# A graph convolution followed by a routed expert network: the first steps of the last stage in another order, with filler matmuls, and 16 instead of 20 edge rows within the pass over x

## What is computed

```python
# x: 12500 x 256, 200000 edges (src, dst, edge_weight), dst sorted
x = x + segment_sum(layernorm(x) @ W [src] * edge_weight, dst) + b      # graph convolution
h = layernorm(x)                                                        # 12500 tokens, D = 256
# routing: ONE vector of logits for all tokens, since B = 1
logits = mean(h, tokens) @ Wr + br            # 8 experts
w = softmax(softmax(logits) * scale)          # scale: capacity
top_w, top_i = top_k(w, 2); top_w = softmax(top_w)
y_e = gelu(h @ W1[e] + b1[e]) @ W2[e] + b2[e] # F = 512; only the two chosen e count
x = x + layernorm(top_w[0] * y_{i0} + top_w[1] * y_{i1} + h)
```

## Time and profile before

| what | value |
|---|---|
| median of 3 runs | 2423.52 us (2422.5 to 2423.78) |
| the profiled execution, its own time | 2425.1 us |
| span of the profile | 2423.2 us |
| PE busy | 2205.2 us (91%) |
| POOL busy | 1617.9 us (67%) |
| DVE, ACT busy | 1030.0 us (43%), 1168.0 us (48%) |
| instructions | 40839 |

### The profile page before, as it was taken

One profiled execution on the slowest core, in us unless ns is written; L12 is line 12 of the kernel. 1 busy time (PEld: TensorE's weight loads), 2 busy tenths in 40 slices (PEclk: granted clock), 3 DMA queues, 4 the chain that ended last, 5 costly groups with the idle time before them and its releaser, 6 DMA issues. The chain is left out here.

```text
span 2423.2 us, 40839 instructions
## 1 busy us (share of the span) xinstructions
PE 2205.2 (91%) x9799; PEld 1696.4 (70%) x9800; DVE 1030.0 (43%) x2967; ACT 1168.0 (48%) x3163; POOL 1617.9 (67%) x1627
## 2 busy tenths in 40 slices
PE   2488899999999999999899999899989979999998
PEld 1367667776667667666677676676766767998897
DVE  7984232322223222232323222322321255889896
ACT  3578667656555545444434343232242116565663
POOL 6777777777777777777777777777777751333432
PEclk9899999999999999999999999999999989999999
DMA  9855565658555655555556556555555542233321
GB/s 374 322 175 155 157 178 166 189 163 271 181 175 171 186 174 177 178 184 168 158 173 189 183 169 191 173 167 187 171 173 179 183 134 83 102 105 127 118 77 59
DMA packets 218864, 414.72 MB, mean 171 GB/s; under 512 B 36227, under 2 KB 130230, under 8 KB 218728
## 3 DMA queue, kind: packets, MB, share of 16 engines
q0 software_dynamic: 75008, 204.90, 28.3%
q1 hardware_dynamic: 143288, 206.10, 26.1%
q10 hardware_dynamic: 432, 2.40, 0.3%
HBM read 332.61 MB, written 80.65 MB: 171 GB/s over the span
## 5 line engine op out<-in xcount | busy, mean ns | idle before, releaser
L533 POOL DMA_INDIRECT G<-xr_d,SRC x1467 | 1395.4, 951 | 447.3 <-issue 296.9
L1024 DVE TENSOR_SCALAR OH<-CST,DL,WR 128x128 f32<-128x128 f32 x1564 | 565.9, 367 | 1279.1 <-PE ps L1337 970.3
L1337 PE MATMUL ps<-G,OH 128*128 x3128 | 743.4, 391 | 104.0 <-DVE OH L1024 75.6
L1337 PEld LDWEIGHTS ps<-G,OH 128*128 128x128 f32 x3128 | 594.2, 194 | 262.5 <-issue 184.4
L1327 PE MATMUL ps<-W2u,H 128*128 128x256 f32 x1792 | 412.3, 389 | 20.3 <-issue 19.3
L1327 PEld LDWEIGHTS ps<-W2u,H 128*128 128x128 f32 x1792 | 344.5, 195 | 88.2 <-issue 41.3
L1316 PE MATMUL ps<-YU,W1u 128*128 128x512 f32 x896 | 394.0, 592 | 1.5 <-issue 1.1
L1316 PEld LDWEIGHTS ps<-YU,W1u 128*128 128x128 f32 x896 | 170.1, 190 | 192.6 <-issue 183.7
L733 ACT ACTIVATE YE<-ps 128x512 f32<-128x512 f32 x112 | 66.8, 596 | 478.4 <-PE ps L1327 478.4
L726 ACT ACTIVATE H<-ps,b1a 128x512 f32<-128x512 f32 x224 | 153.9, 687 | 208.0 <-PE ps L1316 207.7
L612 ACT ACTIVATE OHX<-OHT,WR 128x128 f32<-128x128 f32 x194 | 67.5, 394 | 223.6 <-PE ps L1337 223.6
(11 more groups left out here) (204 smaller groups left out, 2338.5 us busy)
## 6 DMA issues: line engine op xcount, KB each, us to landing
W1u<-in_W SPq DMA_DIRECT2D x56, 512.0 KB
W2u<-in_W SPq DMA_DIRECT2D x56, 512.0 KB
y_d<-YE SPq DMA_DIRECT2D x56, 512.0 KB, 5.4
G<-xr_d,SRC POOLq DMA_INDIRECT x1467, 2.9
x_d<-X SPq DMA_DIRECT2D x98, 128.0 KB, 2.4
yt_d<-YT SPq DMA_DIRECT2D x98, 128.0 KB, 2.3
XR<-in_x SPq DMA_DIRECT2D x97, 128.0 KB, 3.0
XS<-in_x SPq DMA_DIRECT2D x24, 512.0 KB, 19.1
```

The lines of the kernel that those rows point to most:

```text
L533: e.indirect_dma_start(out=G[0:rows(s), s % RING, :], out_offset=None, in_=x if s < FRESH else xr_d, in_offset=bass.IndirectOffsetOnAxis(a ...
L1024: e.tensor_scalar(OH[:, s % OHR, :], iota, DL[:, s:s + 1], WR[:, s + 1:s + 2], ALU.is_equal, ALU.mult).then_inc(s_oh, 1)
L1337: e.matmul(ps[:, 0, 0:D], OH[:, r, :], Gf[:, bass.ds(g + r * D, D)], start=False, stop=True, skip_group_check=True).then_inc(s_main, 1)
```

## The change

Seven edits, in two places of the program.

In the pass over x, `between` puts 3 and 2 rows of edge statistics behind groups 18 and 22 instead of 5 and 4.

In the last stage: ACT's `high(1)` stands in the chain of the routing, behind `XH`; DVE's `low(1)` behind the low parts of W1; ACT's and DVE's steps for `W2h`, `W2l`, `bias_rows` and the first `normal2` come one to several hidden tiles later; PE's first four hidden tiles are done in pairs (high, high, low, low) and no longer all four high parts first; and 6 and 12 filler matmuls of 128x512 (`keep_warm`), whose result is never read, are put on PE before and behind the routing's small matmuls.

```diff
@@ the pass over x
-        between = [1 if 6 <= g < 12 else 5 if g == XBUF else 4 if g == XBUF + LOTS[0] else 1 if g > XBUF else 0 for g in range(NG)]
+        between = [1 if 6 <= g < 12 else 3 if g == XBUF else 2 if g == XBUF + LOTS[0] else 1 if g > XBUF else 0 for g in range(NG)]
@@ ACT
             e.activation(XH[:, :], X1[:, t % 4, :], ACT.Identity, bias=NR[:, t:t + 1], scale=R1[:, t:t + 1]).then_inc(s_xh, 1)
+            high(1)
             e.wait_ge(s_route, 9)
@@
-                    if k == 0 and i in (1, 3):
-                        high_w2(i // 2)
-                    if i == 3 and k + 1 < len(post):
+                    if k == 0 and i in (2, 3):
+                        high_w2(i - 2)
+                    if i == 3 and 1 <= k and k + 1 < len(post):
                         high(k + 1)
-                    if i == 4 and k - 1 in pre_of:
+                    if i == 1 and k == 1 or i == 4 and k - 1 in pre_of:
                         normal2(n)
                         n += 1
-                    if i == 6 and k < len(post):
+                    if i == 6 and 1 <= k < len(post):
@@ DVE
             for h in range(2):
                 low_w1(1, two, h)
+            low(1)
@@
-                    if k == 0 and i in (1, 3):
-                        low_w2(i // 2)
-                    if k == 0 and i == 4:
+                    if k == 0 and i in (2, 4):
+                        low_w2(i // 2 - 1)
+                    if k == 0 and i == 7:
                         bias_rows()
@@
-                    if i == 4 and k + 1 < len(post):
+                    if i == 4 and 1 <= k and k + 1 < len(post):
                         low(k + 1)
@@ PE
+            def keep_warm(n):
+                for _ in range(n):
+                    e.matmul(ps[:, 7, :], ones_r[:, :], YTh[:, 0, 0, :], start=True, stop=True, skip_group_check=True)
@@ behind the last multiplication by Wsb
+            e.wait_ge(s_ye, 2 * UNITS + 2)
+            e.wait_ge(s_yth, 1)
+            keep_warm(6)
@@ behind the transposes of XH
             ins.then_inc(s_tr, 1)
+            keep_warm(12)
@@
-            for i in range(HB):
-                up_high(0, i)
-            for i in range(HB):
-                up_low(0, i)
+            for i in range(0, HB, 2):
+                for j in range(i, i + 2):
+                    up_high(0, j)
+                for j in range(i, i + 2):
+                    up_low(0, j)
```

## The result

The changed kernel takes 2414.97 us (median of 7 runs, 2413.79 to 2418.25) beside 2423.78 (7 runs) for the one before on the same chip: a ratio of 0.9963 (0.9951 to 0.9974), 9.0 us less. On another chip five runs gave 2410.75 beside 2421.71, 0.9959 (0.9945 to 0.9972), 9.9 us less. Gains in us are worked out from the ratio throughout (its interval is some 3 us to either side); the medians alone can differ by 1 us from it. The forecast was 2410.8, 12.7 less: right in direction and within its range, 2.8 to 3.7 us too good.

The account below looks back on a forecast made before the run. POOL's gathers set the pace up to about 1983 us, PE's own work in the steady part from 2020. From the 2423.5 median, 1.8 (pass) and 10.9 (fill) come off: 2410.8 us, range 2408.5 to 2415.5.

Parts of the forecast that it names:

- The pass: Pass over x: fewer edge rows let POOL's stalled gather near 98 us restart 1.8 us earlier; bounds 0 and 3.2.
- both arms: Work needed before PE's `begin` (98.13): ACT's scaling and `AS`, ready at 95.2; PE's first edges and event, 96.3.
- The gather moves with it, 101.33 - 1.8 = 99.5: POOL's gather released by PE's seventh edge row starts 1.8 us earlier, as `begin` does; the floor is 98.15.
- The first rival: The pass gives its whole stall: ACT's arm decides and gives 2.9, at most 3.2 us; total 2409.5; 20%.
- The fill: Start of the last stage: `up(1, 1)` starts at 2008.7 instead of 2019.57, a gain of 10.9 us.
- `W2s` lands at 2001.1 and 2002.6 ..., the evictions ask for it at 2001.2 and 2003.5: In the fill, both `W2s` loads land 4.2 us after issue, before ACT's evictions need them.
- The wait for `YTl` goes: In the fill, PE's 4.06 us wait for `YTl` of group 1 disappears, with `high(1)` and `low(1)` moved earlier.
- I take it that the clock stays at 2.4 GHz: With the fillers, PE's clock does not halve from the routing through the fill; half clock had cost about 3 and 2.6.
- the third rival: The clock falls in the routing anyway; the twelve fillers take 5.1, ending 1.8 late; 2411.9 or 2413.8 us; 17%.
- Then the fill no longer runs its first 16 matmuls at 0.427 each: PE's first fill matmuls avoid half clock, at which one of 512 columns takes 0.427 us; at full clock 0.235.
- The steady loss of 1.5 us or so by late `YTl` stays: Behind the fill, PE keeps its pace of 2.82 us per hidden tile and loses about 1.5 us as before.
- the three things that the prediction named as showing it wrong: Clock 0.50 within the fill; `W2h` waiting for `W2s`; PE waiting over 2 us in total for `Hlo` or `YTl` after 2020.

Follow-up runs that it names:

- pass_only: The kernel before with only the 16 rows in the pass over x (3 and 2 instead of 5 and 4): 2422.02 us beside 2425.54, ratio 0.9989.
- late_g1: The changed kernel with `YTh` and `YTl` of group 1 back at their old places: 2422.06 us, 0.9984 of the kernel before.
- no_warm: The changed kernel without both sets of filler matmuls and their waits: 2413.88 us, 0.9953 of the kernel before.
- no_pairs: The changed kernel with PE's old order in the fill (four high parts, then low parts), on a chip with a slower edge loop: 0.9959 of the kernel before.
- fill_only: The changed kernel with the old 20 rows in the pass, so only the last stage is changed: 2416.43 us, 0.9966 of the kernel before.
- after_again: The repetition: the changed kernel itself on another chip, 2410.75 us beside 2421.71 for the kernel before, ratio 0.9959.
- w2s_first: The changed kernel with SP asking for both `W2s` loads ahead of the `b2s` loads, on a chip with a slower edge loop: 0.9962 of the kernel before.

## Why the prediction was right, and where it was off

- **The pass: both arms right, the way behind them not (1.8 against 2.5).** Both arms came as worked out, and PE's decides. Two steps are off. "The gather moves with it, 101.33 - 1.8 = 99.5" took the way from `begin` to the gather as fixed; it shrank from 3.20 to 2.44, as the clock rose during it. And "Since POOL waited for nothing afterwards, the gain reaches 1983" failed: PE's edges had moved back by 4 us, and in six of the eight profiles POOL waits for it again at gather 76. In the profile after, gather 68 gives 2.51 and 2.12 get past the second stall. The first rival forecast a larger gain with ACT's arm deciding, or PE's event at full clock; the clock did rise, but only at the end of PE's event or behind it, and PE's arm still decides.
- **The fill: 10.9 against 9.4 (9.8 in the repetition; 8.5 and 8.9 against the fill of `pass_only`).** The step that failed is "`W2s` lands at 2001.1 and 2002.6 ..., the evictions ask for it at 2001.2 and 2003.5". It took the median of two loads, 4.2, for both, so that 0.9 us lay between the second landing and its need. That load alone took 4.5 in the same profile, which leaves 0.6, and 6.4 after. Over the ten profiles with that order of loads it took 4.5 and 4.8 in the two with the old fill and 4.6 to 6.8, 5.9 in the mean, in the eight with the new one; whether the change makes it slower is open. The wait of 1.22 is most of the 1.4 missing at `up(1, 0)`. With the load asked for first, the four profiles show no wait above 0.11, and gains of 10.2 to 10.95 over the profile of before.
- **"The wait for `YTl` goes": right**, and it is the edit that carries the fill (`late_g1`: 6.2 of 9.4 us by the profile).
- **The clock: wrong in its state and in its price.** "I take it that the clock stays at 2.4 GHz" holds in the profile after but not in its repetition: the condition of the third rival came in four of nine profiles. Its price did not: the twelve fillers took 4.4 to 4.6 and not 5.1, and the fill started at most 0.6 later and not 1.8. "Then the fill no longer runs its first 16 matmuls at 0.427 each" was put down as part of a gain, where ACT's evictions and `W2s` cover it: `no_warm` has the half clock and loses nothing. (By the prediction's own way of counting, 6.75 us busy at half clock would have cost 3.4, not "about 3".) The Trainium skill's sentence that transposes don't count as busy for the clock as other matmuls do ("TensorE: Matmul & The Clock Gate", "Part 4: PE-mode transpose") is neither shown nor refuted: the falls in the four profiles come at the routing's small matmuls and transposes or right behind them, but no run takes these away, and in the profile after there is no fall with the same instructions.
- **"The steady loss of 1.5 us or so by late `YTl` stays": failed.** It was 2.4 before and 4.4 after (3.5 in the repetition). Over ten profiles with the late `YL` it ranges from 1.5 to 5.3: 2.4 and 2.8 in the two with the old fill, 3.7 in the mean of the eight with the new one. One wait of PE goes with the landing time of its load in nine of these ten profiles. The load is the `YL` issued at 2236.07 before and 2224.02 after. PE waits 0.78 and 0.69 us where it took 6.8, 1.50 where it took 7.5, 1.79 to 1.96 where it took 7.8 to 8.0 (the exception is `no_warm`: 7.0, and only 0.27). Before to after the landing grew by 1.18 and the wait by 1.18; the fall of the clock adds 1.7. Why the load takes longer in most profiles with the new fill is open. That the loss as a whole comes from the late `YL` is shown: asked for a group earlier, it is 0 in all four such profiles.

Two of the three things that the prediction named as showing it wrong did come: `W2h` waited for `W2s`, and PE waited more than 2 us in total (2.3) for `YTl` after 2020. The time still fell within the range, whose high end was set to hold several such misses together.

The total of the runs also moves with the edge loop: a gather takes 1.2527 to 1.2571 us in the mean from profile to profile on the usual chips, and times 1494 that is 6.6 us. That is more than what lies between 9.0 and 9.9, or between either and the 12.7 of the forecast, so the total alone could not have told which step was off.

## What to carry to other kernels

A gain at the start of a long chain whose pace another engine sets arrives at its end, so it is read at one place, but behind the last stall that the change touches: gather 100 here, not gather 68. A load that lands just in time in one profile is not in time: ask how much earlier the buffer and the address were free, and issue it there; moving two loads on SP gave half as much as the whole change. A stretch at half clock is worth its price only where PE is what the others wait for; price it by the next engine's start, not by PE's busy time.

## What the runs showed of the hardware

- A wait of PE for the late `YTl` of 1.96 us (in the profile after and in `no_pairs`) was followed by matmuls at granted clock 0.50 for 3.4 us, so that it cost 3.7 in all. Waits of 1.79 to 1.88 at the same place (`fill_only`, `after_again`, `w2s_first`, `late_g1`) left the clock at 1.00. In the fill of `late_g1` the clock fell within a wait of 2.38, which came 0.7 us behind 2.18 idle, and stayed at 0.50 for 5.7 us of work. The same program also shows different clocks in the same place: 1.00 throughout the routing in the profile after, 0.50 for 3.4 us in its repetition.
- A load of 512 KB took 3.3 (`pass_only`, `YL` of group 1) to 8.0 us from issue to landing in the last stage. The DMA share was 0.46 during one of 3.4 before and 0.88 during the 6.4 of the second `W2s` after; but it was also 0.83 and 0.85 while that load took 4.8 in `pass_only` and 4.6 in `no_warm`, so the share alone does not tell how long a load takes.
